# Graph attention: target rows as two float32r parts, two one-pass products a tile, and one wait per gather pair

## What is computed

```python
x = layernorm(x)
xl = (x @ W_l).reshape(n, H, C)              # n = 6250, H = 4 heads, C = 64
xr = (x @ W_r).reshape(n, H, C)
feat = xl[src] + xr[dst]                     # one row per edge
feat = where(feat >= 0, feat, 0.2 * feat)
logits = einsum('ehc,hc->eh', feat, att)
ex = exp(logits - segment_max(logits, dst)[dst])
alpha = ex / (segment_sum(ex, dst)[dst] + 1e-16)
out = segment_sum(alpha[:, :, None] * xl[src], dst)
```

## Time and profile before

| | |
|---|---|
| median of 3 runs | 2407.22 us (2406.8 to 2407.28) |
| the profiled execution | 2405.22 us, span 2403.4 us |
| TensorE matmul busy | 2098.9 us (87%) |
| TensorE weight loads busy | 1766.2 us (73%) |
| VectorE busy | 1559.2 us (65%) |
| ScalarE busy | 1209.4 us (50%) |
| GpSimd busy | 1348.4 us (56%) |
| mean granted TensorE clock | 0.914 of 2.4 GHz |

### The profile page before, as it was taken

How to read it: one execution, slowest core, us unless ns; L and a number is a source line. 1 busy time by engine, 2 the same in 40 slices (tenths; PEclk the granted TensorE clock), 3 DMA queues, 4 the chain that set the end, 5 groups by cost and what they waited for, 6 DMA issues and landing times. The chain is left out here.

```text
span 2403.4 us, 45705 instructions
## 1 busy us (share of the span) xinstructions
PE 2098.9 (87%) x9585; PEld 1766.2 (73%) x9586; DVE 1559.2 (65%) x3459; ACT 1209.4 (50%) x3043; POOL 1348.4 (56%) x1265
## 2 busy tenths in 40 slices
PE   2978999999999999999999999449568359999993
PEld 1766888888888888888888887238458348888882
DVE  6756888888888888888888888964555301111110
ACT  2434667667666666667667667335321012322220
POOL 3347777766767677677776772750017734444442
PEclk9989999999999999999999999659655579999996
DMA  7557666556656656656565662540443356665664
GB/s 210 187 191 191 179 165 173 167 162 172 168 163 173 166 164 171 165 167 171 165 167 167 167 168 69 151 150 0 126 123 88 102 155 143 149 141 140 144 142 127
DMA packets 264254, 365.71 MB, mean 152 GB/s; under 512 B 50491, under 2 KB 201684, under 8 KB 264076
## 3 DMA queue, kind: packets, MB, share of 16 engines
q0 software_dynamic: 73984, 154.20, 27.0%
q1 hardware_dynamic: 174384, 194.13, 26.8%
q10 hardware_dynamic: 15836, 16.81, 2.2%
HBM read 306.42 MB, written 64.88 MB: 154 GB/s over the span
## 5 line engine op out<-in xcount | busy, mean ns | idle before, releaser
L788 POOL DMA_INDIRECT ring<-xl_rows,a_idx x928 | 924.3, 996 | 378.3 <-issue 338.2
L1098 PE MATMUL a_f_ps<-a_xr_w,a_hot_n 128*128 128x268 f32 x1856 | 577.0, 393 | 23.2 <-DMA ring<-xl_rows,a_idx 20.4
L1100 PE MATMUL a_f_ps<-ring,ident 128*128 128x264 f32 x1856 | 566.7, 387 | 0.0
L1111 PE MATMUL a_o_ps<-ring,a_hot_e 128*128 128x264 f32 x1856 | 494.2, 390 | 2.8 <-ACT a_hot_e L867 1.5
L966 DVE SCALAR_TENSOR_TENSOR a_pos<-a_f_ps,att_ext 128x528 f32<-128x528 f32 x464 | 325.5, 702 | 151.6 <-PE a_f_ps L1100 151.2
L1098 PEld LDWEIGHTS a_f_ps<-a_xr_w,a_hot_n 128*128 128x128 f32 x1856 | 346.3, 191 | 86.3 <-issue 27.7
L1100 PEld LDWEIGHTS a_f_ps<-ring,ident 128*128 128x128 f32 x1856 | 354.0, 191 | 66.9
L1111 PEld LDWEIGHTS a_o_ps<-ring,a_hot_e 128*128 128x128 f32 x1856 | 344.3, 190 | 65.5 <-issue 6.5
L976 DVE TENSOR_REDUCE a_lg<-a_pos 128x8 f32<-128x528 f32 x464 | 322.8, 696 | 0.8
L1855 POOL DMA_INDIRECT acc_rows<-ring,x_idx x112 | 173.9, 1553 | 260.4 <-DVE ring L1953 153.4
L984 DVE TENSOR_TENSOR ring<-ring (+1 forms) x464 | 315.9, 681 | 0.0
(11 more groups left out here) (314 smaller groups left out, 2195.1 us busy)
## 6 DMA issues: line engine op xcount, KB each, us to landing
a_xr_w<-xr_rows SPq DMA_DIRECT2D x464, 134.0 KB, 2.2
a_rel_bc<-rel_rows SPq DMA_DIRECT2D x116, 256.0 KB, 4.3
x_w<-in_L_ffn_W_dram SPq DMA_DIRECT2D x56, 512.0 KB, 4.5
ring<-xl_rows,a_idx POOLq DMA_INDIRECT x928
ring<-disp_rows SPq DMA_DIRECT2D x56, 257.0 KB, 2.7
xr_rows<-xr_sb SPq DMA_DIRECT2D x50, 134.0 KB, 1.9
xl_rows<-xl_sb SPq DMA_DIRECT2D x50, 132.0 KB, 1.8
j_xl<-xl_rows SPq DMA_DIRECT2D x25, 264.0 KB, 2.8
```

The lines of the kernel that those rows point to most:

```text
L788: nc.gpsimd.indirect_dma_start(xl_e[:, p * T + 2 * h + u, :], None, k.xl_rows, bass.IndirectOffsetOnAxis(ap=idx[:, p, 2 * h + u:2 * h + u ...
L1098: nc.tensor.matmul(f_ps[:, g, u, 0:XRW], hot_n[:, j % 2, 2 * g + u, :], xr_w[:, h % XR, :], start=True, stop=False)
L1100: last = nc.tensor.matmul(f_ps[:, g, u, 0:XW], k.ident[:, :], xl_e[:, p * T + 2 * h + u, :], start=False, stop=True)
L1111: last = nc.tensor.matmul(o_ps[:, hh % 2, 0:XW], hot_e[:, j % 2, 2 * g + u, :], xl_e[:, pp * T + 2 * hh + u, :], start=(u == 0), stop=(u = ...
```

## The change

The target rows are stored and loaded as two parts. ScalarE copies a row of `xr_sb` to the type float32r (the high part), VectorE subtracts it from the row and stores the rest as float32r (the low part). `xr_rows` and `xr_w` are twice as wide. The one-hot `hot_n` gets the type float32r, and each f32 product of it becomes two products, with the high and with the low part, that add up in the same PSUM region. The rings of the projected rows have eight places instead of four, and SyncE's store waits for the low part. Before a gather pair GpSimd waits for one count, `sum_done` (`f_done` in the first 32 units), and at a chunk's first pair for `idx_ready` too. Elsewhere semaphores of the edge stage are merged (`compared`, `odd_ready` and `slots_ready` into `patterned`; `gates_ready` and `words_ready` into one). The core of the diff:

```diff
+F32R = mybir.dt.float32r
+PARTS = 2
...
     RING = 4
+    ROWS = 8
...
-                    sp.wait_ge(xr_full, t + 1)
+                    sp.wait_ge(low_ready, t + 1)
...
-                    sp.dma_start(k.xr_rows[bass.ds(row, P), :], xr_sb[:, s, :]).then_inc(stored[s], 16)
+                    sp.dma_start(k.xr_rows[bass.ds(row, P), :], parts[:, s].rearrange("p a w -> p (a w)")).then_inc(stored[s], 16)
...
                     nc.vector.tensor_reduce(xr_sb[:, s, XW:XRW], heads_of(g_sb[:, b, :]), AX.X, ALU.add).then_inc(xr_full, 1)
+                    if not isinstance(t, int) or t >= 1:
+                        low_part(t - 1, (s - 1) % ROWS)
+
+                def low_part(t, s):
+                    dve.wait_ge(high_ready, t + 1)
+                    nc.vector.tensor_tensor(parts[:, s, 1, :].bitcast(F32R), xr_sb[:, s, :], parts[:, s, 0, :], ALU.subtract).then_inc(low_ready, 1)
...
                     nc.scalar.copy(xr_sb[:, s, 0:XW], xr_ps[:, s % 2, 0:XW]).then_inc(x_ready, 1)
+                    if not isinstance(t, int) or t >= 1:
+                        high_part(t - 1, (s - 1) % ROWS)
+
+                def high_part(t, s):
+                    act.wait_ge(xr_full, t + 1)
+                    nc.scalar.copy(parts[:, s, 0, :].bitcast(F32R), xr_sb[:, s, :]).then_inc(high_ready, 1)
...
-        xr_w = sb("a_xr_w", [P, XR, XRW])
+        xr_w = sb("a_xr_w", [P, XR, PARTS, XRW])
...
-        hot_n = sb("a_hot_n", [P, 2, QT, P])
+        hot_n = sb("a_hot_n", [P, 2, QT, P], F32R)
...
                 def gather(c, p, h):
-                    wait_past(pool, sum_done, c * NU + (h - RING + 1))
-                    wait_past(pool, f_done, c * NU + (h - LANDS + 1))
-                    pool.wait_ge(idx_ready, c + 1)
+
+                    if isinstance(c, int) and c * NU + h < RING:
+                        wait_past(pool, f_done, c * NU + (h - LANDS + 1))
+                    else:
+                        pool.wait_ge(sum_done, c * NU + (h - RING + 1))
+                    if h == 0:
+                        pool.wait_ge(idx_ready, c + 1)
...
                     for u in range(2):
-                        nc.tensor.matmul(f_ps[:, g, u, 0:XRW], hot_n[:, j % 2, 2 * g + u, :], xr_w[:, h % XR, :],
-                                         start=True, stop=False)
+                        for a in range(PARTS):
+                            nc.tensor.matmul(f_ps[:, g, u, 0:XRW], hot_n[:, j % 2, 2 * g + u, :], xr_w[:, h % XR, a, :].bitcast(F32R),
+                                             start=(a == 0), stop=False)
                         last = nc.tensor.matmul(f_ps[:, g, u, 0:XW], k.ident[:, :], xl_e[:, p * T + 2 * h + u, :],
                                                 start=False, stop=True)
...
-    k.xr_rows = dram("xr_rows", [COLS, XRW])
+    k.xr_rows = dram("xr_rows", [COLS, PARTS * XRW])
```

More of the change, by code:

```diff
@@ L492, in project_nodes @@
         zt_sb = sb("zt_sb", [P, 2, 2, P])
-        xl_sb = sb("xl_sb", [P, RING, XW])
-        xr_sb = sb("xr_sb", [P, RING, XRW])
+        xl_sb = sb("xl_sb", [P, ROWS, XW])
+        xr_sb = sb("xr_sb", [P, ROWS, XRW])
+        parts = sb("xr_parts", [P, ROWS, PARTS, XRW])
         f_sb = sb("f_sb", [P, 2, XW])
@@ L502, in project_nodes @@
         mm_done, x_ready, f_ready, g_ready, xr_full = sem("n_mm"), sem("n_x"), sem("n_f"), sem("n_g"), sem("n_xr_full")
-        stored = [sem(f"n_stored{s}") for s in range(RING)]
+        high_ready, low_ready = sem("n_high"), sem("n_low")
+        stored = [sem(f"n_stored{s}") for s in range(ROWS)]
         with nc.Block() as block:
@@ L519, in _ @@
                         sp.dma_start(out[h * T:(h + 1) * T], rows[:, 0:NCH, :]).then_inc(k.fixed, 16)
-                tiles(sp, NTP, RING, RING, store)
+                tiles(sp, NTP, ROWS, ROWS, store)
                 sp.wait_ge(k.fixed, 16 * (2 + 2 * H))
-                for s in range(RING):
-                    sp.wait_ge(stored[s], 32 * len(range(s, NTP, RING)))
+                for s in range(ROWS):
+                    sp.wait_ge(stored[s], 32 * len(range(s, NTP, ROWS)))
             @block.gpsimd
@@ L530, in both_sides @@
                     nc.gpsimd.tensor_tensor(f_sb[:, s % 2, :], xl_sb[:, s, :], xr_sb[:, s, 0:XW], ALU.add).then_inc(f_ready, 1)
-                tiles(pool, NTP, RING, RING, both_sides)
+                tiles(pool, NTP, ROWS, ROWS, both_sides)
             @block.vector
@@ L557, in first_half @@
                 def first_half(t, s):
-                    normalise(t + AHEAD, (s + AHEAD) % RING)
+                    normalise(t + AHEAD, (s + AHEAD) % ROWS)
                     self_logits(t, s, lambda: measure(nc, k, t + LN_HALF))
                 def second_half(t, s):
-                    normalise(t + AHEAD, (s + AHEAD) % RING)
+                    normalise(t + AHEAD, (s + AHEAD) % ROWS)
                     self_logits(t, s)
-                tiles(dve, TURN, RING, RING, first_half)
+                tiles(dve, TURN, ROWS, ROWS, first_half)
                 for t in range(TURN + LN_HALF, NTP):
```

49 lines of the change are left out of this document (26 added, 23 removed).

## The result

The changed kernel takes **2332.5 us** (median of 4 runs, 2331.5 to 2337.8) against 2407.2 us (4 runs, 2406.8 to 2407.3): a ratio of 0.9695 with a 95% interval of 0.9678 to 0.9711. The forecast was 2326 us in a range of 2285 to 2385. The profiled execution took 2331.6 us, span 2329.5 us.

The account below looks back on a forecast made before the run. The prediction took TensorE as the bound, with GpSimd next: -84 us in attention and +3 in the projection make -81, from 2405.2 to 2324, and with the median's 2 us 2326, in a range of 2285 to 2385.

Parts of the forecast that it names:

- What bounded the kernel: Steady attention stretch: TensorE is the bound, six f32 products of 0.45 us in a unit of 2.835 us.
- The one-pass product: Target rows' product: four passes of 0.113 us replace 0.90 us a unit; rival that a pass is no quicker, 8%.
- GpSimd's floor: Attention chunk: 32 gathers of 0.997 us plus 0.304 us pause each, 41.6 us a chunk, 2.60 a unit.
- GpSimd as the next wall: Attention stage: once TensorE is relieved, GpSimd's 41.6 us a chunk is the larger limit, against 40.8.
- VectorE's and TensorE's 40.8 us a chunk: Attention chunk: VectorE's softmax part of 17.49 us plus ten other units, TensorE's, falling from 27.81 to 23.3 us.
- The 0.7 us added per chunk: Attention chunk: charge for hand-overs between three engines, raising 41.6 to 42.3 us.
- The gathers slow down: Rival, 5%: denser VectorE or DMA load lengthens GpSimd's gathers, about 2450 us at 1.16; message product's effect priced at 3 us.
- The gain per unit: Attention stage: a unit falls by 0.191 us to 2.644; over 438 units 84 us.
- the projection's 3 us: Projection stage: cast and subtraction hidden behind TensorE; +3 us, between 0 and +10, mostly the last tile's longer tail.
- One wait: Before each gather pair on GpSimd: worth 0, up to some 10 us if register work were not hidden.
- the doubled loads: SyncE's target-row loads of 268 KB instead of 134: taken as 0, DMA share from 0.60 to 0.83.
- The signals: Signs in the new profile: passes 0.11 us apart, L966 every 2.64 us, pauses 0.30, DMA share about 0.8, L530 2.1 or less.

Follow-up runs that it names:

- The third-pass kernel: The changed kernel with the low part's product issued twice, three one-pass products where there are two: 2354.9 us, ratio 0.9787.
- the kernel with the weights in PSUM: The changed kernel, but VectorE's message product reads its weights from PSUM, filled by one more ScalarE copy a chunk: 2297.3 us, ratio 0.9548.
- the four others: Changed kernel with three waits, high part alone or weights in PSUM, and kernel before with one wait: 2639.8, 2636.8, 2628.7, 2635.4 us under the disturbance.

## Why the prediction was right

**What bounded the kernel: right.** A busy TensorE was a full one. Six f32 products of 0.45 us and a unit of 2.835 us are borne out by what happened when 0.4 us of them went.

**The one-pass product: the size slightly off.** The prediction took 0.113 us. In the changed kernel's timeline of TensorE (start us, us) two passes stand in front of each product with the source rows:

```profile
700.82 0.51 PE L1125 MATMUL a_f_ps<-a_xr_w,a_hot_n 128*128 128x268 f32 x2
701.16 0.61 PE L1127 MATMUL a_f_ps<-ring,ident 128*128 128x264 f32 x2
701.41 0.60 PE L1125 MATMUL a_f_ps<-a_xr_w,a_hot_n 128*128 128x268 f32 x2
701.85 0.61 PE L1127 MATMUL a_f_ps<-ring,ident 128*128 128x264 f32 x2
702.30 1.05 PE L1138 MATMUL a_o_ps<-ring,a_hot_e 128*128 128x264 f32 x4
```

From 701.16 to the first L1138 at 702.30 pass 1.14 us, in which two f32 products (0.89) and two passes run: 0.12 a pass. The third-pass kernel, 0.12 us longer over the same stretch, gives the same. TensorE's chunk is therefore 45.3 - 16 x (0.90 - 4 x 0.123) = 38.8 us and not 38.1, which mattered nothing, as the prediction had said for any pass under 0.17: GpSimd's floor is above it. Two records a product before and two passes now are the same number of instructions (x1856), so the gain comes only from the time that each takes.

**GpSimd as the next wall: right, and it was the step that carried the forecast.** The pauses are 0.305 us throughout, TensorE waits before its first product for gathers, and halving the gathers moves the chunk to the other limit.

**VectorE's and TensorE's 40.8 us a chunk: right.** The kernel with half the gathers runs at 40.8, as 17.5 and 23.3 us, the very two terms of the sum. Only the owner of the second differs: the prediction gave the other ten units to TensorE, and there VectorE hardly waits for it (0.7 us a chunk).

**The 0.7 us added per chunk: right in size, wrong in cause.** The prediction took 42.3 us as 41.6 plus "hand-overs between three engines". The chunk is 16 x 2.648 = 42.4. But no hand-over costs anything, since GpSimd never waits longer than its smallest gap. The 0.7 is 32 x (1.019 - 0.997): longer gathers. That a charge for one thing came to the size of another was luck: without the 0.7 the same sum comes out some 19 us lower, at 2307. Before, GpSimd moved in step with TensorE, and its gathers started mostly at harmless moments; between 300 and 1300 us, 58 of 708 started within 0.55 us after a message product's start. As the wall it runs free through VectorE's cycle of 2.65 us, and 140 of 755 do.

**The gathers slow down: the step that failed, though the rival as a whole did not come true.** The prediction dismissed the message product's effect with one pair of rows, the gather of 802.35 at 0.95 us with the message product of 802.91 across its end, and priced the rest at 3 us. That gather had *started before* the message product. The row that spoke the other way, the gather of 1.26 us at 835.61, was given no cause. Its cause stood in the same timeline of VectorE of the kernel before:

```profile
835.36 0.68 DVE L984 TENSOR_TENSOR ring<-ring  x1
```

The gather starts 0.25 us after this message product does. The prediction's 3 us scaled the lengthening with how dense VectorE works, and what changed was how often a gather starts inside the product. Measured against the kernel with the weights in PSUM, the hold costs the changed kernel 35 us; the gathers there are shorter by 0.058 us, 51 us in all, but the next limit keeps the rest. Of the lengthening, 0.022 x 2 x 437 = 19 us are new with the change; the kernel before had the rest too, hidden behind TensorE, nearly half of it in 18 gathers of 1.60 to 1.67 us that started 0.10 to 0.17 us ahead of a message product.

**The gain per unit: right.** 2.835 - 2.646 = 0.189 us against 0.191. The profiled execution fell by 2405.2 - 2331.6 = 73.6 us where the sum had 81. By the starts of L966 and L992, the 437 units from the 27th to the last took 1236.8 us before and 1158.7 now: 78 us less where the sum had 84, or 0.179 a unit on average against 0.189 in the middle. The 27th unit starts 4.5 us later than before; 3.4 of this the projection cost when it was measured alone, against +3 in the sum, so this term is right too.

**How the projection's 3 us came about: half as thought.** The prediction had VectorE's subtraction hidden behind TensorE, and the 3 us mostly in the last tile's tail. The first gather of the attention starts 4.0 us later (168.6 us before, 172.5 now). The tail from the last of GpSimd's adds to it grew by 1.9 us, from 5.6 to 7.5, as said. But the other 2.1 us are there at 96 us already, in the half of the stage in which VectorE also takes statistics. Busy time there, 62 to 94 us, of the kernel before and of the changed one:

```profile
62.00:94.00 32.00, 32.00 (x160) 26.53 (x159) 26.37 (x64) 14.99 (x48) 11.94 (x17) 1.00 0.65 218
62.00:94.00 32.00, 32.00 (x154) 24.76 (x153) 32.00 (x77) 20.59 (x62) 14.48 (x16) 1.00 0.73 260
```

VectorE has no room left (26.4 of 32 us busy, then 32.0), and the adds come 2.11 us apart where they came every 2.02. In the second half they stay 2.01 to 2.02 apart: there the subtraction is hidden. The prediction's own terms for VectorE also add up to more than its 2.16 us a tile, namely 3 x 0.46 + 0.42 + 0.42 = 2.22. Groups by line in the changed kernel, 106 to 160 us, against the earlier trace rows:

```profile
L536 POOL TENSOR_TENSOR f_sb<-xl_sb,xr_sb 128x264 f32<-128x264 f32 x25 | 19.2, 768 | 37.7 <-ACT xr_sb L601 37.7
L548 DVE TENSOR_SCALAR z_sb<-ring,ln_mean,ln_rstd 128x256 f32 (+1 forms) x25 | 18.4, 734 | 0.8 <-DVE ln_rstd L451 0.6
L607 ACT CAST xr_parts<-xr_sb 128x268 fp32r<-128x268 f32 x25 | 10.6, 424 | 0.0
...
L564 DVE TENSOR_TENSOR xr_parts<-xr_sb,xr_parts 128x268 fp32r<-128x268 f32 x24 | 10.3, 428 | 0.0
```

The cast and the subtraction are as long as costed. But the normalise has grown from 464 to 734 ns, and in the first half it takes 835. VectorE's and GpSimd's timelines show with what it meets:

```profile
120.64 0.94 DVE L548 TENSOR_SCALAR z_sb<-ring,ln_mean,ln_rstd 128x256 f32 x1
...
122.64 0.41 DVE L548 TENSOR_SCALAR z_sb<-ring,ln_mean,ln_rstd 128x256 f32 x1
...
120.68 0.74 POOL L536 TENSOR_TENSOR f_sb<-xl_sb,xr_sb 128x264 f32<-128x264 f32 x1 [1.26 <-ACT xr_sb L601]
122.78 0.88 POOL L536 TENSOR_TENSOR f_sb<-xl_sb,xr_sb 128x264 f32<-128x264 f32 x1 [1.35 <-ACT xr_sb L601]
```

The normalise now starts where GpSimd adds. At 120.64, with the add 0.04 us behind it, it takes 0.94 us instead of 0.41. At 122.64, with the add 0.14 us behind, it takes 0.41 and the add 0.88 instead of 0.74. That one of the two is blocked fits the same section of the Trainium skill. No run takes this meeting away, so what it costs of the 2.1 us is not shown.

**One wait, and the doubled loads: 0 each, right.** Both have their own kernels: the waits change nothing, and halving the loads gains nothing.

**The signals.** L992 comes every 2.65 us (2.64 said), the first six units of a chunk take 17.5 us as before by its starts, the DMA share is 0.77 at 231 GB/s (0.8 said), and GpSimd's adds in the projection are 2.1 us apart or less. The passes' records don't start 0.11 us apart: the first of two starts 0.03 us after the record before it and the second 0.32 later, so a pass can only be timed over a longer stretch, as above.

## What to carry to other kernels

When a full engine is relieved, work out the next engine's floor with its smallest gap included (mean length plus gap, not busy time), since this number decides the result. Here the engine that became the wall lost its phase with the others, and the length measured while it was in step was too short: look how its instructions fare at every phase before using their mean. Where GpSimd is that wall, see what VectorE instruction a GpSimd instruction can *start* in; moving one small operand to PSUM brought 35 us here, on top of the 75 of the whole change. A stage whose halves have different limits is summed by halves, as the chunk's two parts were; the projection's first half was not, and it was there that VectorE filled up.

## What of the hardware was unexpected

- A gather that starts inside VectorE's message product of 0.68 us is held until that ends (1.41 us at 0.10 us into it, 1.25 at 0.26), but one that starts 0.55 us into it or later isn't (0.96). Of the 280 in the changed kernel that started up to 0.9 us before it, 273 were not held (0.96) and seven were (1.66 to 1.67). With the second operand in PSUM there is no hold. A `tensor_scalar` over SBUF of 0.42 us holds too (1.16).
- A one-pass float32r product of 268 columns costs 0.12 us at the full granted clock, against 0.225 for each record of an f32 product.
- For a time every kernel took 10 to 14% longer (2642 us for the kernel before, 2629 to 2640 for the four others), with waits of up to 6 us put down to `remote`, at a mean granted clock of 0.92 to 0.97 in the steady stage. Later, on a chip of the same number in the record, the kernel before took 2406.8 us, so the cause is not shown to be the chip.
